# Second attention head of two graph layers written out in front of its loop: the order of its dot products, its down-projection, its weight roundings and its edge keys

## The reference

```python
def gat_layer(x, W1, a_s, a_d, b1, W2, ...):
    h = (x @ W1).reshape(256, 8, 768)
    alpha_s, alpha_d = (h * a_s).sum(-1), (h * a_d).sum(-1)
    e = leaky_relu(alpha_s[src] + alpha_d[dst], 0.2)
    alpha = softmax over the edges of each dst
    out = segment_sum(h[src] * alpha, dst)
    out = elu(out.reshape(256, 8 * 768) + b1)
    second unit: the same with one head on out, W2 (6144 x 768)
```

## Time and profile before

| what | us |
|---|---|
| median of 3 executions | 1358.67 (1357.21 to 1361.64) |
| the profiled execution | 1354.77 |
| its span, first to last instruction | 1352.9 |
| TensorE busy | 1281.9 |
| VectorE busy | 995.6 |
| ScalarE busy | 642.6 |

### The profile page before, as it was taken

One profiled execution on the slowest core, in us unless ns is written; L12 is line 12 of the kernel. 1 busy time (PEld: TensorE's weight loads), 2 busy tenths in 40 slices (PEclk: granted clock), 3 DMA queues, 4 the chain that ended last, 5 costly groups with the idle time before them and its releaser, 6 DMA issues.

```text
span 1352.9 us, 21068 instructions
## 1 busy us (share of the span) xinstructions
PE 1281.9 (95%) x7775; PEld 1138.7 (84%) x7775; DVE 995.6 (74%) x1633; ACT 642.6 (47%) x832; POOL 209.4 (15%) x160
## 2 busy tenths in 40 slices
PE   6989999997989999997898999999999999999997
PEld 5779999975879999976687888898888898888886
DVE  6978888987778888985777756666556665556676
ACT  5656656545456665644444434433334333344342
POOL 0023444441023444440000000000000000000200
PEclk9989999998989999998999999999999999999999
DMA  9575566653455556643334644445544455443640
GB/s 335 163 259 171 171 191 212 178 145 98 172 151 192 171 171 196 213 126 117 106 129 163 224 164 155 155 170 189 183 155 155 157 184 190 166 155 140 189 128 33
DMA packets 103926, 227.38 MB, mean 168 GB/s; under 512 B 16758, under 2 KB 34998, under 8 KB 103888
## 3 DMA queue, kind: packets, MB, share of 16 engines
q1 hardware_dynamic: 72972, 192.43, 40.4%
q10 hardware_dynamic: 20980, 31.78, 8.2%
q0 software_dynamic: 9936, 2.66, 2.1%
HBM read 216.56 MB, written 10.29 MB: 168 GB/s over the span
## 4 chain that ended last, share of the span: by engine, by line
PE 82%; DVE 11%; ACT 3%; issue 2%; DMA 1%; DVEq 0%; ACTq 0%; SPq 0%
PE bank L443 81%; DVE w_lo L1335 3%; ACT w_hi L991 1%; DVE stats L1373 1%; PE bank L539 1%; PE bank L482 1%; DMA w_in<-L_gnn_W_root 1%; DVE h_lo L1335 1%; DMA x_sb<-x 1%; DVE neg_b L1338 0%; DVE xT_lo L1335 0%; DVE x_sb L1335 0%; DMA scores_b<-table 0%; DVE neg_b L1579 0%; ACT xT_hi L991 0%
## 5 line engine op out<-in xcount | busy, mean ns | idle before, releaser
L1335 DVE TENSOR_TENSOR w_lo<-w_in,w_hi 128x2304 fp32r<-128x2304 f32 (+4 forms) x162 | 396.7, 2477 | 66.0 <-ACT w_hi L991 65.9
L991 ACT ACTIVATE w_hi<-w_in 128x2304 fp32r<-128x2304 f32 (+4 forms) x162 | 328.3, 2063 | 228.2 <-PE bank L443 198.7
L443 PE MATMUL bank<-w_hi,xT_hi 128*128 128x384 f32 (+3 forms) x942 | 323.5, 343 | 4.0 <-DVE xT_lo L1335 3.0
L443 PE MATMUL bank<-w_lo,xT_hi 128*128 128x384 f32 (+3 forms) x942 | 307.0, 338 | 0.0
L443 PE MATMUL bank<-w_hi,hid_hi 128*128 128x512 f32 (+3 forms) x858 | 295.1, 344 | 4.6 <-DVE hid_lo L1335 4.4
L443 PE MATMUL bank<-w_lo,hid_hi 128*128 128x512 f32 (+3 forms) x858 | 272.6, 338 | 0.0
L443 PE MATMUL bank<-w_hi,xT_lo 128*128 128x384 f32 (+3 forms) x942 | 245.2, 339 | 0.0
L443 PE MATMUL bank<-w_hi,hid_lo 128*128 128x512 f32 (+3 forms) x858 | 225.6, 339 | 0.0
L443 PEld LDWEIGHTS bank<-w_hi,xT_hi 128*128 128x128 f32 (+1 forms) x942 | 176.9, 188 | 30.5 <-issue 4.6
L443 PEld LDWEIGHTS bank<-w_hi,hid_hi 128*128 128x128 f32 (+1 forms) x858 | 162.5, 189 | 41.4 <-issue 5.9
L1880 DVE SCALAR_TENSOR_TENSOR neg_b<-bank,rinv,neg_b 128x512 f32<-128x512 f32 (+1 forms) x136 | 77.5, 612 | 153.0 <-PE bank L443 153.0
(11 more groups left out here) (250 smaller groups left out, 1535.2 us busy)
## 6 DMA issues: line engine op xcount, KB each, us to landing
w_in<-L_gnn_W_rel SPq DMA_DIRECT2D x68, 1152.0 KB, 5.8
w_in<-L_gnn_W SPq DMA_DIRECT2D x66, 1152.0 KB, 6.1
table<-zrow SPq DMA_DIRECT2D x4, 2304.0 KB, 16.5
scores_b<-table ACTq DMA_DIRECT2D x34, 256.0 KB, 3.0
a_bc<-L_gnn_a_src ACTq DMA_DIRECT2D x18, 384.0 KB, 3.8
a_bc<-L_gnn_a_dst ACTq DMA_DIRECT2D x18, 384.0 KB, 5.1
key_row<-key_rows ACTq DMA_DIRECT2D x16, 256.0 KB
w_in<-ffn_out SPq DMA_DIRECT2D x4, 864.0 KB, 6.9
```

Source lines behind the costliest of these rows:

```text
L443: return pe.matmul(out, lhsT, rhs, start=start, stop=stop, **kw)
L991: act.activation(out, ps, func, **kw).then_inc(mark, 1)
L1335: return dve.tensor_tensor(out, a, b, op)
```

## The change

Head 1 of both attention layers is taken out of the loops of VectorE and ScalarE, which now run over heads 2 to 6, and has an order of its own on three engines.

TensorE (`rest_of_second`): the twelve steps of head 0's down-projection run over the first half of the weights for both row tiles, then over the second half. Six steps stand before `spread`, four between `spread` and `turn`, two between `turn` and `attend`.

VectorE: head 1's four dot products follow the first head's last remainder directly. The remainder of the second half of head 0's W2 chunk (`first_down`) comes behind them, before the scores. `batch_firsts(b - 1)`, the first head's edge keys, and the remainder of the first half of head 2's W1 chunk (n0 + 4) stand behind the remainder of alpha. Head 1's own `batch_firsts` stays between `unit` and `remainder`.

ScalarE: in layer 0, rounding the second half of head 0's W2 chunk goes behind the evictions of head 1's h. `load_key` of head 1 goes from before alpha's eviction to behind the rounding of the second half of head 2's W1 chunk.

```diff
+                def rest_of_second():
+                    steps = [(m, k) for k0 in (0, 3) for m in range(M) for k in range(k0, k0 + 3)]
+                    def first_down(i0, i1):
+                        for m, k in steps[i0:i1]:
+                            down(0, n0 + 3, m * K + k, m * K + k + 1)
+                    first_down(0, 6)
+                    spread(1 + 9 * layer)
+                    first_down(6, 10)
+                    turn(1 + 9 * layer)
+                    first_down(10, 12)
+                    parts_kept(1 + 9 * layer)
+                    attend()
...
-                rest_of(1)
+                rest_of_second()
...
+                    if second_head and layer == 0:
+                        high(n0 + 3, c0 + 4, 0, parts=(1,))
                     if not first_head:
                         high(h * 2 + (n0 + 2), h * 2 + (c0 + 3), 1, parts=(0,))
...
                     attend(u, ahead)
                     if not first_head:
                         high(h * 2 + (n0 + 2), h * 2 + (c0 + 3), 1, parts=(1,))
+                        if second_head:
+                            load_key(1 + HEADS * layer)
...
-                    elif first_head:
-                        if layer == 0:
-                            high(n0 + 3, c0 + 4, 0, parts=(1,))
-                    else:
+                    elif not first_head:
                         high(h * 2 + (n0 + 3), h * 2 + (c0 + 4), 0)
...
-                with act.Fori(1, HEADS - 1) as h:
+                head(1, lambda: load_heads(layer, 2), second_head=True)
+                with act.Fori(2, HEADS - 1) as h:
                     head(h, lambda: tables(h))
...
                         tile_dots(u, m, junk[:, :], together)
                     tile_low(u, 0, together)
+                meanwhile()
                 dve.wait_ge(src_row, u + 1)
...
+                    def first_down():
+                        low(n0 + 3, 0, parts=(1,))
+                    scores(h + 9 * layer, layer, ahead, begun=first_head and layer == 0,
+                           meanwhile=first_down if second_head else lambda: None)
+                    if second_head:
+                        batch_firsts(b - 1)
+                        low(h * 2 + (n0 + 2), 1, parts=(0,))
...
-                        if first_head:
-                            low(n0 + 3, 0, parts=(1,))
-                        batch_firsts(b)
+                        if last_head:
+                            batch_firsts(b)
...
-                with step.loop(1, HEADS - 1, 9 + layer) as h:
+                head(1, second_head=True)
+                with step.loop(2, HEADS - 1, 9 + layer) as h:
```

More of the change, by code:

```diff
@@ L1045, in gat, with head @@
                 c0, n0, b0 = C_GAT[layer], NTH_GAT[layer], layer * HEADS
-                def head(h, ahead, first_head=False, last_head=False):
+                def head(h, ahead, first_head=False, second_head=False, last_head=False):
                     u = h + 9 * layer
@@ L1431, in tile_low, with scores @@
                 low_of(h_lo[:, m, :], h_sb[:, m, :], h_hi[:, m, :], h_low)
-            def scores(u, layer, ahead, together=False, begun=False):
+            def scores(u, layer, ahead, together=False, begun=False, meanwhile=lambda: None):
                 if not begun:
@@ L1475, in gat, with head @@
                 step(ts(flat(mask[:, :, :]), flat(cnt[:, layer, :, :]), 0.0, ALU.is_equal, NONE, mul))
-                def head(h, first_head=False, last_head=False):
+                def head(h, first_head=False, second_head=False, last_head=False):
                     b = h + HEADS * layer
@@ L1482, in head, with ahead @@
                         ahead = second_count if layer == 0 else lambda: None
+                    elif second_head:
+                        def ahead():
+                            pass
                     else:
@@ L1485, in ahead @@
                             low(h * 2 + (n0 + 2), 1, parts=(0,))
-                    scores(h + 9 * layer, layer, ahead, begun=first_head and layer == 0)
+                    def first_down():
[5 more added lines that the diff above has]
+                        low(h * 2 + (n0 + 2), 1, parts=(0,))
                     if not first_head or layer == 0:
```

## The result

The changed kernel takes 1350.7 us (median of 9 runs, 1346.9 to 1354.25), the kernel before on the same chip 1357.05 (9 runs, 1353.89 to 1361.64): a ratio of 0.9952, 95% interval 0.9936 to 0.9968. That is 6.35 us less, where 7.9 had been forecast. The profiled execution took 1351.34 us with a span of 1349.5, against 1354.77 and 1352.9 before; the granted clock is 0.986 in both.

A forecast was written before the change was run, and what follows sets the result against it. It took TensorE's wait for VectorE's dots before head 1's spread, then VectorE's queue behind alpha, as the bound. Layer 0's 4.6 and layer 1's 3.3 us sum to 7.9, giving 1350.8 us; range 1347.2 to 1355.5.

The forecast's parts named there:

- (c): Loads late in both layers, or the block behind alpha 2 us dearer: gain of 2 to 4 us left; 10 in 100.
- (a): TensorE keeps its whole gain because VectorE catches up in its waits: 11.2 us, 1347.5; 8 in 100.
- (b): The new TensorE waits bring the clock down, 1.5 to 1.8 us per low stretch: 1352.3 to 1354.3; 17 in 100.
- the wait for the remainder: Layer 0, behind head 1's spread: TensorE's seventh step stands 1.8 us, from 78.2 to 80.0, for VectorE's moved weight remainder.
- just in time: Layer 0, ScalarE: weight rounding ahead of the exponentials, at 80.11 for its DMA, ends at 82.23; exponentials must be free at 82.3.
- the loads: SP's weight loads move with the remainders freeing the buffer; a late one costs 0, at worst 0.3 to 0.5 us per layer.
- nothing: Head 1 written out of the loop: saves a loop turn on two engines, with only 0.27 us idle before its first dot.
- TensorE's 1.6 us in hand: A low clock in front of attend would be hidden, since TensorE has 1.6 us in hand there.
- Rival (d): GpSimd's batches start later, from 34.5 us a batch the gain is lost, at 36 it is 1364.8; 5 in 100.
- the hole: TensorE's wait for VectorE's third dot before head 1's spread, 6.74 us in layer 0, 5.86 in layer 1; gone in layer 0.
- VectorE's queue: Keys and two weight remainders behind alpha's remainder cut attend's gain of 6.3 us to 4.6 in layer 0.
- The prediction's price of the low stretches: A low-clock stretch costs 1.5 us in layer 0, to 1.8 us; hidden before attend, in full behind head 2's spread.

The follow-up runs named there:

- e5: The changed kernel again, unaltered, measured beside three follow-up kernels: 1349.82 us, ratio 0.9955 to the kernel before.
- e7: The changed kernel with the first batch's keys in VectorE's gap ahead of aT_lo and the dots behind the weight remainder: 1346.97 us, ratio 0.9932 to the kernel before.
- e6: The changed kernel with only the first batch's edge keys moved, into the gap between alpha and aT_lo: 1348.95 us, ratio 0.9944 to the kernel before.
- e8: e3 without TensorE's halves: keys behind aT_lo, dots second, down-projection in its old order; 1351.1 us, ratio 0.9962 to the kernel before.
- e4: The changed kernel without the first batch's key compares in both layers, GpSimd's adds of it going to spill rows: 1381.08 us, ratio 1.0165 to the kernel before.
- e9: The kernel before with 26 multiplications by zero in TensorE's wait ahead of head 1's spread: 1352.9 us, ratio 0.9974 to the kernel before.
- e1: The kernel before with only TensorE's down-projection ordered by weight halves: 1351.23 us, ratio 0.9958 to the kernel before.
- e3: The changed kernel with head 1's dots back behind the weight remainder and ScalarE's rounding in its old place: 1349.74 us, ratio 0.9945 to the kernel before.
- e11: e7 with the dots ahead of the remainder in layer 1 alone: 1346.5 us, ratio 0.9924 to the kernel before.
- e12: e7 without the halves, head 0's down-projection in its old order: 1351.67 us, ratio 0.9958 to the kernel before.

## Why the prediction was right, and where its terms were off

**The sum, 7.9 against 6.4 to 6.7.** That the forecast time, 1350.8, was met to 0.1 us is luck: the nine executions of the kernel before lie 1.6 us below the three from which the forecast started, and the gain is 1.55 us smaller. Nor does the sum of the chances contain "the better half of (c)": 0.84 is about the forecast, (a) and (b) together (0.85), and all of (c) lies less than 4.1 us below 1358.67. At full clock, in e5, the two distances are 3.28 and 3.80 us shorter, 7.1 together, where 4.6 and 3.3 had been forecast. In the profile taken first, 3.40 and 2.88.

**Layer 0 up to the units: right within 0.6 us.** `spread` 78.00 (forecast 77.7), the wait for the remainder 1.23 (1.8), alpha done at 84.53 + 0.62 = 85.15 (84.7), `attend` 87.78 (87.25), units 95.13 (94.9). What made alpha late is a step that the forecast called "just in time": ScalarE's weight rounding in front of the exponentials waited for its load until 80.90 instead of 80.11, and VectorE stood 0.58 us for them.

```profile
80.90 2.13 ACT L1007 ACTIVATE w_hi<-w_in 128x2304 fp32r<-128x2304 f32 x1 [4.42 <-DMA w_in<-L_gnn_W]
```

```profile
83.46 0.43 DVE L1359 CUSTOM_DVE_ANT_0 scores_b<-prob,cnt 128x256 f32<-128x256 f32 x1 [0.58 <-ACT prob L1007]
```

**Layer 0 behind the units: the mis-sized term is the loads,** put at "0, at worst 0.3 to 0.5 per layer". The half of W2 issued at 91.89 landed at 99.3, 7.4 us later; the forecast had 5.9, 7.2 at the longest. It cost 1.59 and 0.72 on ScalarE, 0.55 and 0.30 on VectorE, and head 2's `spread` came 110.39 - 95.13 = 15.26 behind the units instead of 113.62 - 99.49 = 14.13: 1.1 us of the 4.6. In e7 the same load is on time and TensorE doesn't wait there. Why it takes 7.4 to 9.9 us in the kernels with the dots first (change, e5, e6) and under 6 in e7 is not settled. With the dots first the remainder that frees the other half of the buffer ends at 79.8 instead of 76, so the loads behind it move. But that can't be all: e8 has the dots second, and there the load issued at 92.39 was rounded only at 99.35, 7.0 us later, behind a wait of 1.15. What the tables by stretches show is that the load starts slowly: 90, 165 and 249 GB/s in the three microseconds from 92 on in the changed kernel, 169, 359 and 415 in e7. That the DMAs of GpSimd and ScalarE are the cause was only argued.

**Layer 1: a little under-estimated at full clock, 3.8 for 3.3.** In the first profile it was 2.9. Most of the difference lies ahead of alpha, where the written-out head saves more than the "nothing" of the forecast: the waits of 0.28 and 0.16 in front of the first and the third dot (384.96 and 387.09 in the kernel before) are gone, and alpha is done 13.74 us behind the first step instead of 14.14. The prediction held that a clock fall in front of `attend` would be hidden by TensorE's 1.6 us in hand. It was not: it cost 0.92 (e5). `turn` comes later, so aT_hi does, VectorE waits 2.32 instead of 1.38 for it, and the keys and remainders queued behind it all move. TensorE's time in hand at head 2 is no shelter for what VectorE waits for.

**Rival (b)** was in part there: in the first profile the clock fell behind the wait of 2.46 at head 2 and cost 1.56, in full, as said. e5's profile has no fall, and its median stands no better against the kernel before (0.9955, and 0.9952 the first time). So the rival is a matter of executions and not a case of its own. **Rival (a)** is out: the waits of 1.4 to 2.9 us at head 2 are there in both profiles. **Rival (c)** was there in layer 0 alone. Two of the signs by which the prediction said that it would be wrong did appear in the first profile, the low clock behind a new wait (b) and VectorE's waits of 0.55 and 0.30 for a rounding behind alpha (c); the time held since each of them cost about 1 to 1.6 us and not the whole of its rival. **Rival (d)** did not happen, but e4 shows it is real (the prediction's own numbers, 466 against 456, leave it 10 us of reserve and not 8); in the changed kernel layer 1's batches take (592.38 - 395.98) / 7 = 28.1 us each, less than a head's 30.5. GpSimd's timeline, start of the first and of the eighth, answering to the earlier trace rows:

```profile
395.98 2.43 POOL L390 TENSOR_TENSOR value<-first,ones 128x4 f32<-128x4 f32 x1 [85.29 <-DVE again L1356]
...
592.38 1.62 POOL L390 TENSOR_TENSOR value<-first,ones 128x4 f32<-128x4 f32 x1 [2.96 <-DMA table<-value,row_i]
```

**What the argument gave too little weight.** The reasons named were the hole and VectorE's queue. e9 shows that nearly half of the 7.1 us in the two distances can be had from the clock alone: holding it with zeros, with the hole left as it was, gives 3.4 there and 3.7 in the median. The new order gives a further 80.63 - 76.95 = 3.7 (e9 to e5, both without a low stretch). The prediction's price of the low stretches, 1.5 and 1.8 us, was right; what it did not see is that they are half of the gain and don't need the new order. And the parts do not add up: halves alone 5.3 (e1), keys moved without the halves 5.4 (e8), both 6.7 (e3). Either one shortens or covers the same wait and saves part of the same clock. The third part, the dots first, shows no gain in either layer and costs up to 2.4 us in layer 0 once the keys are out of the way. A forecast part by part, each against the kernel before, would have counted the same microseconds twice; this one held since it walked through all of them in one timeline.

## What to carry to other kernels

A long wait of TensorE can cost twice, its own length and the clock behind it; try a few idle multiplications in it first, since they show in one run how much of a reorder's gain is only the clock. When work is pushed off the way to a result, put it into the next gap of its engine and not behind the gap: with TensorE's halves in place and the dots second, the kernel with the keys in front of aT_lo was faster than that with the keys behind it by 1.8 us going by the ratios and 2.8 by the medians (e3 to e7, on different chips, with intervals that overlap), and by 1.4 us in layer 0's distance. Where a late load stood in the way, the same move brought 0.9 us, not separable from nothing (e5 to e6). And when an engine's order moves the step that frees a load's buffer, follow the loads to where they are wanted, with more than the median of their landing times.

## What the runs showed of the hardware that was not expected

- Whether the clock falls is not told by the length of the wait. A wait of about 1.85 us in layer 1 brought it down in the change, e4, e6 and e11 and not in e5; one of 3.37 did not in e8, one of 3.35 did in e12. 26 multiplications by zero (5.79 us) in waits of about 6 us kept it up both times.
- Indirect adds of 128 values to 128 neighbouring rows took about 12 us each (49.7 for four, e4). Those of the same batch to the rows of the edges stood 4.5 to 7.6 us apart in the changed kernel.
- Low stretches far from any edit move with the execution: one profile had one at 730 us, another none there but one at 1281. Medians of kernels that differ by 2 us could not be told apart with 5 to 11 executions. A distance inside one trace leaves such stretches out, but it is one execution and can mislead in its own way, as e8's did.
